# Probabilities times context in three rounded terms, with the sum of exponentials by accumulating transfers

## The chip, the cores and the metric

The kernel runs on one core of one Trainium2 chip. The metric is device time in microseconds; the time before is the median of three runs.

## The reference

Eight batches of 56 tokens with 128 channels attend to 1500 context rows each, with 16 heads of 64, and an expert network follows. All is float32.

```python
x = x + xattn(layernorm(x), ctx, mask, Wq, Wkv, Wout, bout)
#   q = x @ Wq; k, v = split(ctx @ Wkv); 16 heads
#   dots = q k^T * SCALE - (1 - mask[query]) * 1e6
#   out = softmax(dots) v @ Wout + bout
x = x + ffn(layernorm(x), w1, b1, w2, b2)
#   one expert per batch: gelu(x @ w1[e] + b1[e]) @ w2[e] + b2[e]
```

## The kernel before

The weights are folded: the query's and the key's of a head into w_qk, the value's and the output's into w_vo. So attention works on the context itself. A batch has Q = 16 x 56 = 896 query columns `qk`; its 1500 context rows are 12 tiles of 125 (TM, MT).

Scores are made in three rounded terms. A float32 value is cast to float32r (the high part, `ctxt_hi`, `qk_hi`), and the rest is subtracted (`ctxt_lo`, `qk_lo`, on GpSimd). TensorE takes high x high, high x low and low x high, each in two halves c of 448 columns: six matmuls per tile (L398) into one of two PSUM buffers ps_s. Before that, from tile 2 on, ScalarE has written the shift of each query (its maximum and the mask) there (`seed`, L612), so that ScalarE's exponential (L605) gives bounded probabilities `ex`, in a ring of six tiles. For tiles 0 and 1 the shift is a matmul (L412). Probabilities times context (L426, `probs_ctx`) is two float32 matmuls per tile, in the accumulators ps_a. VectorE adds the tiles to `ex_sum` one by one (`add_tile`, L762), and TensorE sums that over partitions with a matrix of ones (L441).

One call of `iteration(b)` on each engine does batch b and in its cracks other work. Step t has three places (t, 0), (t, 1), (t, 2) on TensorE: in the scores of tile t ahead of the third term, behind the scores, and inside the probabilities of tile t-2, which stand last in a step. In the first two steps those are tiles 10 and 11 of the batch before. At the places of MAX_AT stand 21 matmuls (L434) over the next batch's scores, whose maxima VectorE takes (L765). They, the sums, the shift and the expert network are "jobs": each writes one of two PSUM banks ps_x in turn, and waits until the one of two jobs earlier has been read (`job_free`). Every second iteration (a pair of batches done) also has the output projection (L453, at (5, 2)), the norm, and the expert network (L473 at (8, 1), L482 at (11, 2)) of the pair before. Its gelu is exponential, cap, logarithm, exponential and product, on ScalarE in steps 10 and 11 (L655, L661, L663) and on VectorE (L863, at (11, 1)). A loop of three rounds runs iterations 1 to 6 in twos; batch 0 and batch 7 stand outside. Batch 7's second half of a pair follows at the end by itself.

Each engine takes its instructions in the order written. VectorE's per step is `drain((t, 0))`, `between`, the addition of tile t-1, `drain((t, 1))`, `drain((t, 2))`; it also casts the next batch's context (`ctxt_hi_chunk`, L782, in steps 0 and 1) and queries (`qk_hi_part`, L786). In steps 3 and 4 it takes the sums (`drain_sum`, L793) with ScalarE's inverses (L635). GpSimd's only waits are for the high parts. SyncE loads the context twice per batch, as rows (`ctx_sb`, two buffers) and transposed (`ctxt_raw`, one buffer, reloaded when `ctxt_lo` is done).

## Time and profile before

| | us |
|---|---|
| median of three runs | 407.91 (405.58 to 409.17) |
| the profiled execution | 405.75 |
| its span on the core | 403.9 |

The profile is one execution. Its page lists busy time by engine (1), the span in 40 slices with TensorE's granted clock and the transfers (2), the DMA queues (3), the chain of work that ended last, followed back from the last instruction (4), and the costliest groups by line with the wait before them (5). A line number is that of the kernel. PE is TensorE, DVE VectorE, ACT ScalarE, POOL GpSimd, SPq the queue of SyncE. Where several records stand in one row (x6), the duration is that of all of them. A float32 matmul leaves two records, a rounded one leaves one. Matmuls overlap in the records, so the distance from start to start is what one costs.

### The profile page before, as it was taken

To read this page: it belongs to the slowest core of one execution; us is meant where nothing else is said; L and a number is where in the kernel's file an instruction comes from. 1 tells how busy PE (TensorE), PEld (TensorE's weight loads), DVE (VectorE), ACT (ScalarE), POOL (GpSimd) and SP (SyncE) were. 2 spreads that over 40 slices of the span, in tenths; PEclk is the share of its full clock that TensorE was granted. 3 is DMA by queue.
4 is the path that set the end of the run, shared out by engine and by line. 5 is a ranking of instruction groups with operands and counts; after the bars stand their busy time and mean duration, and the time that the engine had idled before them with its cause. 6 is when DMAs were issued, how large, how long until landed. Compare 5 with 4: busy or idle time off the path is not lost.

```text
span 403.9 us, 5555 instructions
## 1 busy us (share of the span) xinstructions
PE 390.0 (97%) x1721; PEld 281.2 (70%) x1721; DVE 302.8 (75%) x490; ACT 206.0 (51%) x274; POOL 57.6 (14%) x47
## 2 busy tenths in 40 slices
PE   7998999999999999999999999999999999999995
PEld 6665666767675877767776877667766777676684
DVE  4889678877887689877887689787887686365443
ACT  3546354565457444665455454565357444746431
POOL 0603400600060000600060001500150000000000
PEclk9999999999999999999999999999999999999999
DMA  7660020040005000042004000160011001100000
GB/s 252 210 199 21 2 76 1 12 142 0 2 4 148 2 2 2 25 155 81 0 18 135 0 0 0 43 193 26 0 35 42 0 0 53 57 2 0 3 2 3
DMA packets 20661, 19.62 MB, mean 49 GB/s; under 512 B 904, under 2 KB 17576, under 8 KB 20648
## 3 DMA queue, kind: packets, MB, share of 16 engines
q1 hardware_dynamic: 20648, 19.45, 15.7%
q8 instruction: 8, 0.13, 0.1%
q14 instruction: 5, 0.04, 0.0%
HBM read 19.21 MB, written 0.23 MB: 48 GB/s over the span
## 4 chain that ended last, share of the span: by engine, by line
PE 90%; DVE 5%; ACT 2%; issue 1%; DMA 1%; SPq 0%; ACTq 0%; DVEq 0%
PE ps_a L426 35%; PE ps_s L398 28%; PE ps_x L434 10%; PE ps_x L453 4%; PE ps_x L441 3%; PE ps_a L373 2%; PE ps_x L473 2%; PE ps_x L482 2%; PE ps_s L412 2%; DMA ex<-in_wk_t 1%; DVE log_sum L793 1%; DVE ctxt_hi L782 1%; ACT inv_sum L635 1%; PE ps_s L528 1%; PE ps_x L412 1%
## 5 line engine op out<-in xcount | busy, mean ns | idle before, releaser
L426 PE MATMUL ps_a<-ex,ctx_sb 125*128 125x448 f32 x384 | 172.1, 541 | 0.0
L605 ACT ACTIVATE ex<-ps_s 125x896 f32<-125x896 f32 x96 | 88.0, 917 | 117.4 <-PE ps_s L398 91.3
L765 DVE TENSOR_REDUCE chunk_max<-ps_x 128x1 f32<-128x500 f32 x168 | 111.3, 674 | 32.6 <-PE ps_x L434 29.5
L434 PE MATMUL ps_x<-ctxt_hi,qk_hi 128*128 128x500 f32 x168 | 88.5, 530 | 6.3 <-DVE log_sum L793 3.6
L426 PEld LDWEIGHTS ps_a<-ex,ctx_sb 125*128 125x128 f32 x384 | 71.4, 189 | 27.5 <-issue 21.6
L762 DVE TENSOR_TENSOR ex_sum<-ex_sum,ex 125x896 f32<-125x896 f32 x80 | 86.6, 1083 | 4.6 <-ACT ex L605 4.6
L398 PE MATMUL ps_s<-qk_hi,ctxt_hi 128*125 128x448 f32 x192 | 87.2, 535 | 0.0
L612 ACT COPY ps_s<-shift_row 125x896 f32<-125x896 f32 x80 | 72.9, 911 | 9.9 <-DVE shift_row L882 7.8
L398 PEld LDWEIGHTS ps_s<-qk_hi,ctxt_hi 128*125 128x125 f32 x192 | 35.8, 187 | 35.5 <-issue 35.1
L398 PE MATMUL ps_s<-qk_hi,ctxt_lo 128*125 128x448 f32 x192 | 57.3, 379 | 0.0
L1008 POOL TENSOR_TENSOR qk_lo<-qk,qk_hi 128x448 fp32r<-128x448 f32 x16 | 23.7, 1483 | 218.9 <-DVE qk_hi L786 218.1
L398 PE MATMUL ps_s<-qk_lo,ctxt_hi 128*125 128x448 f32 x192 | 54.8, 366 | 0.0
L434 PEld LDWEIGHTS ps_x<-ctxt_hi,qk_hi 128*128 128x128 f32 x168 | 31.5, 188 | 26.6 <-issue 9.2
L398 PEld LDWEIGHTS ps_s<-qk_hi,ctxt_lo 128*125 128x125 f32 x192 | 35.6, 186 | 6.9 <-issue 2.6
L398 PEld LDWEIGHTS ps_s<-qk_lo,ctxt_hi 128*125 128x125 f32 x192 | 35.6, 185 | 3.4
L1014 POOL TENSOR_TENSOR ctxt_lo<-ctxt_raw,ctxt_hi 128x500 fp32r<-128x500 f32 x24 | 32.0, 1347 | 11.3 <-DVE ctxt_hi L782 11.3
L782 DVE CAST ctxt_hi<-ctxt_raw 128x500 fp32r<-128x500 f32 x24 | 23.7, 1018 | 0.0
L793 DVE TENSOR_TENSOR log_sum<-ps_x,inv_sum 128x448 f32<-128x448 f32 x16 | 9.3, 619 | 18.6 <-ACT inv_sum L635 18.6
L453 PEld LDWEIGHTS ps_x<-w_vo,att_n 128*128 128x128 f32 (+1 forms) x160 | 18.1, 170 | 1.5 <-issue 1.2
L453 PE MATMUL ps_x<-w_vo,att_n 128*128 128x128 f32 (+1 forms) x160 | 18.6, 275 | 0.0
L629 ACT ACTIVATE log_sum<-ps_x 128x448 f32<-128x448 f32 x16 | 8.7, 542 | 10.7 <-PE ps_x L441 10.6
L648 ACT ACTIVATE logv<-veps 128x1 f32<-128x1 f32 (+2 forms) x7 | 1.4, 204 | 24.7 <-DVE veps L828 22.5
(79 smaller groups left out, 263.3 us busy)
## 6 DMA issues: line engine op xcount, KB each, us to landing
ctxt_raw<-in_ctx_t SPq DMA_DIRECT2D x8, 750.0 KB, 7.4
ctx_sb<-in_ctx SPq DMA_DIRECT2D x8, 750.0 KB
w_sb<-in_w SPq DMA_DIRECT2D x4, 512.0 KB, 3.8
w_sb<-in_w SPq DMA_DIRECT2D x8, 256.0 KB, 4.4
ex<-in_wq_t SPq DMA_DIRECT2D x2, 256.0 KB, 3.9
ex<-in_wk_t SPq DMA_DIRECT2D x2, 256.0 KB, 4.8
att_n<-in_wv_t SPq DMA_DIRECT2D x1, 512.0 KB, 5.9
att_n<-in_w_out SPq DMA_DIRECT2D x1, 512.0 KB, 7.1
```

Source lines behind the costliest of these rows:

```text
L398: mm = nc.tensor.matmul(dst[c], a[:, u, rows], q[:, u, chunks[c]], start=(n == 0 and not seed), stop=(n == 2 and seed), skip_group_check=seed)
L426: mm = nc.tensor.matmul(ps_a[:, c, 0:CH], ctx_sb[0:MT, u, t, :], ex[0:MT, t % RING, c * CH:(c + 1) * CH], start=(t == 0), stop=(t == TM - 1))
L434: nc.tensor.matmul(bank[:, 0:MC], qk_hi[:, u, t * P:(t + 1) * P], ctxt_hi[:, u, k * MC:(k + 1) * MC], start=True, stop=True).then_inc(job_ ...
L453: mm = nc.tensor.matmul(bank[pair.tokens(), 0:D], att_n[:, h, pair.tokens()], w_vo[:, h, :], start=(h == 0), stop=(h == HEADS - 1))
L605: nc.scalar.activation(half(ex[0:MT, slot, :]), src, ACT.Exp, scale=SCALE).then_inc(ex_ready, 1)
L612: nc.scalar.copy(ps_s[0:MT, t % 2, :, 0:CH], half(shift_row[0:MT, :])).then_inc(seeded, 1)
L762: nc.vector.tensor_tensor(dst, left, ex[0:MT, t % RING, :], ALU.add).then_inc(ex_summed, 1)
L765: nc.vector.tensor_reduce(chunk_max[:, k, t:t + 1], filled()[:, 0:MC], AX.X, ALU.max).then_inc(job_free, 1)
L782: nc.vector.tensor_copy(ctxt_hi[:, b.parity, k * MC:(k + 1) * MC], ctxt_raw[:, k * MC:(k + 1) * MC]).then_inc(ctxt_hi_ready, 1)
L793: nc.vector.tensor_tensor(log_sum[:, cols], bank[:, 0:CH], inv_sum[:, cols], ALU.mult).then_inc(job_free, 1)
L1008: nc.gpsimd.tensor_tensor(qk_lo[:, b.parity, cols], b.pick(qk)[:, cols], qk_hi[:, b.parity, cols].bitcast(F32), ALU.subtract).then_inc(qk_ ...
L1014: nc.gpsimd.tensor_tensor(ctxt_lo[:, b.parity, cols], ctxt_raw[:, cols], ctxt_hi[:, b.parity, cols].bitcast(F32), ALU.subtract).then_inc(c ...
```

## The change

For nine of the twelve tiles (SPLIT) probabilities times context is done in rounded terms like the scores. ScalarE takes the exponential of such a tile a second time, into a float32r ring `ex_hi`; VectorE subtracts it from the first (`low_part`, `ex_lo`); GpSimd splits the context rows of these tiles once per batch into `ctx_hi` and `ctx_lo` (`split_ctx`, a copy and a subtraction for four tiles in step 8 of the iteration before, and for five in step 1). TensorE then does six rounded matmuls in place of two float32 ones.

The sum is no longer made by eleven additions. Tiles 0, 1 and 2 are written into `ex_first` (two copies, by parity), which are three accumulators. GpSimd issues a transfer for each of the tiles 3 to 10 (in the last batch 3 to 8) that adds the tile to the accumulator t % 3 (`add_by_dma`), after the transfer before it on that accumulator has landed. VectorE adds tile 11 and the other two accumulators to the third, at (0, 1), (1, 0) and (1, 2) of the next iteration. Tiles 3 to 11 go through a ring of four, and an exponential waits for the transfer that reads its slot. The full 128 partitions are transferred, so both are cleared at the start.

The query cast moves from VectorE to ScalarE, behind the exponential of tile 0. The context casts stand all in step 0. `shifts` is one place earlier. In MAX_AT the place (3, 2) is no longer used, and the tables of GpSimd's work (CTXT_LO_AT, QK_LO_AT) are changed: its queue now waits for the exponentials of each step. `hid` and its two companions lie in `w_qk`'s memory.

```diff
-    RING = 6
-    assert D == P and MT * TM == M and QT * P == Q and MC * KM == M and E == B and TM % RING == 0
-    CTXT_LO_AT, QK_LO_AT = [2, 6, 7], [2, 3]
+    RING, ACCS, LAST_DMA = 4, 3, 10
+    assert D == P and MT * TM == M and QT * P == Q and MC * KM == M and E == B and ACCS < RING < LAST_DMA < TM
+    SPLIT = [1, 2, 4, 5, 6, 7, 8, 9, 10]
+    PARTS = 3
+    assert len(SPLIT) % PARTS == 0 and 0 not in SPLIT and TM - 1 not in SPLIT
+    CTXT_LO_AT, QK_LO_AT = [5, 6, 7], [2, 9]
+    CTX_SPLIT_AT = [8, 1]
     REFINE_AT, ATT_N_AT, Z_AT = (3, 3), (4, 3), (6, 2)
-    QK_HI_AT = (0, 0)
-    CTXT_HI_AT = [(0, 1), (0, 2), (1, 0)]
+    CTXT_HI_AT = [(0, 0), (0, 1), (0, 2)]
+    SUM_PARTS_AT = [(0, 1), (1, 0), (1, 2)]
+    LAST_SUM_PARTS_AT = [(9, 2), (10, 0), (10, 2), (11, 0)]
     MAX_AT = [
-        [(1, 1), (1, 2), (2, 0), (2, 1), (2, 2), (3, 2), (4, 0), (4, 2), (5, 0), (5, 2), (6, 0),
-         (6, 1), (6, 2), (7, 0), (8, 0), (8, 2), (9, 0), (9, 1), (9, 2), (10, 1), (10, 2)],
-        [(1, 1), (1, 2), (2, 0), (2, 1), (2, 2), (3, 2), (4, 0), (4, 2), (5, 0), (5, 2), (6, 0),
-         (6, 2), (7, 0), (7, 1), (8, 0), (8, 1), (8, 2), (9, 1), (9, 2), (10, 1), (10, 2)],
+        [(1, 1), (1, 2), (2, 0), (2, 1), (2, 2), (4, 0), (4, 1), (4, 2), (5, 0), (5, 1), (6, 0),
+         (6, 2), (7, 0), (7, 1), (8, 0), (8, 2), (9, 0), (9, 2), (10, 0), (10, 1), (10, 2)],
+        [(1, 1), (1, 2), (2, 0), (2, 1), (2, 2), (4, 0), (4, 1), (4, 2), (5, 0), (5, 2), (6, 0),
+         (6, 2), (7, 0), (7, 2), (8, 0), (8, 2), (9, 0), (9, 2), (10, 0), (10, 1), (10, 2)],
     ]
...
-        ex = sb("ex", [P, RING, Q])
-        ex_sum = sb("ex_sum", [P, 2, Q])
+        ex_first = sb("ex_first", [P, 2, ACCS, Q])
+        ex_ring = sb("ex_ring", [P, RING, Q])
+        ex_hi = sb("ex_hi", [P, PARTS, Q], F32R)
+        ex_lo = sb("ex_lo", [P, PARTS, Q], F32R)
+        ctx_hi = sb("ctx_hi", [P, len(SPLIT), D], F32R)
+        ctx_lo = sb("ctx_lo", [P, len(SPLIT), D], F32R)
...
+        ADDS = [sum(t % ACCS == j for t in range(ACCS, LAST_DMA + 1)) for j in range(ACCS)]
+        DVE_SUMS = TM - 1 - LAST_DMA + ACCS - 1
+        LAST_BATCH_DMA = 8
...
+        def last_dma(b):
+            return LAST_BATCH_DMA if b.off == B - 1 else LAST_DMA
+        def sums_of(b):
+            return TM - 1 - last_dma(b) + ACCS - 1
+        def ex(b, t):
+            return ex_first[:, b.parity, t, :] if t < ACCS else ex_ring[:, (t - ACCS) % RING, :]
+        def parts_free(eng, b, t):
+            n = SPLIT.index(t)
+            if n >= PARTS:
+                eng.wait_ge(pv_done, b.at(TM, SPLIT[n - PARTS] + 1))
+            elif b.i is not None or b.off > 0:
+                eng.wait_ge(pv_done, b.later(-1).at(TM, SPLIT[n - PARTS] + 1))
+        def dma_added(eng, b, t):
+            eng.wait_ge(ex_added[t % ACCS], b.at(16 * ADDS[t % ACCS], 16 * (t // ACCS)))
...
-                for c in range(2):
-                    if c == 1 and between is not None:
-                        between()
-                    mm = nc.tensor.matmul(ps_a[:, c, 0:CH], ctx_sb[0:MT, u, t, :], ex[0:MT, t % RING, c * CH:(c + 1) * CH],
-                                          start=(t == 0), stop=(t == TM - 1))
+                if t in SPLIT:
+                    n = SPLIT.index(t)
+                    pe.wait_ge(ex_hi_ready, b.at(len(SPLIT), n + 1))
+                    if t in (SPLIT[0], SPLIT[4]):
+                        pe.wait_ge(ctx_lo_ready, b.at(2, 1 if t == SPLIT[0] else 2))
+                    for k, (w, e) in enumerate([(ctx_hi, ex_hi), (ctx_lo, ex_hi), (ctx_hi, ex_lo)]):
+                        if k == 1 and between is not None:
+                            between()
+                        if k == 2:
+                            pe.wait_ge(ex_lo_ready, b.at(len(SPLIT), n + 1))
+                        for c in range(2):
+                            mm = nc.tensor.matmul(ps_a[:, c, 0:CH], w[0:MT, n, :], e[0:MT, n % PARTS, c * CH:(c + 1) * CH],
+                                                  start=False, stop=False)
+                else:
+                    for c in range(2):
+                        if c == 1 and between is not None:
+                            between()
+                        mm = nc.tensor.matmul(ps_a[:, c, 0:CH], ctx_sb[0:MT, u, t, :], ex(b, t)[0:MT, c * CH:(c + 1) * CH],
+                                              start=(t == 0), stop=(t == TM - 1))
...
-                wait(act, pv_done, b.at(TM, t - RING + 1))
-                wait(act, ex_summed, b.at(TM - 1, max(t - RING, 1)) if t >= RING else b.at(TM - 1, t - RING + 1))
-                nc.scalar.activation(half(ex[0:MT, slot, :]), src, ACT.Exp, scale=SCALE).then_inc(ex_ready, 1)
+                if t >= ACCS + RING:
+                    act.wait_ge(pv_done, b.at(TM, t - RING + 1))
+                    dma_added(act, b, t - RING)
+                elif t >= ACCS and (b.i is not None or b.off > 0):
+                    act.wait_ge(pv_done, b.at(TM, 0))
+                    before = b.later(-1)
+                    last = max(s for s in range(ACCS, TM) if (s - t) % RING == 0)
+                    if last <= LAST_DMA:
+                        dma_added(act, before, last)
+                    else:
+                        act.wait_ge(ex_summed, before.at(DVE_SUMS, last - LAST_DMA))
+                nc.scalar.activation(half(ex(b, t)[0:MT, :]), src, ACT.Exp, scale=SCALE).then_inc(ex_ready, 1)
+            def high_part(b, t):
+                parts_free(act, b, t)
+                nc.scalar.activation(half(ex_hi[0:MT, SPLIT.index(t) % PARTS, :]), ps_s[0:MT, t % 2, :, 0:CH], ACT.Exp,
+                                     scale=SCALE).then_inc(ex_hi_ready, 1)
+            def qk_hi_part(b):
+                wait(act, scores_ready, b.at(TM, -TM))
+                nc.scalar.copy(qk_hi[:, b.parity, :], b.pick(qk)).then_inc(qk_hi_ready, 1)
...
+                if t - 2 in SPLIT:
+                    act.wait_ge(ex_hi_ready, b.at(len(SPLIT), SPLIT.index(t - 2) + 1))
...
+                    if t in SPLIT:
+                        high_part(b, t)
                     if t == 1 and b.off > 0:
                         att_out(b.later(-1))
+                    if t == 0 and prepare:
+                        qk_hi_part(b.later(1))
...
+            def sum_parts(b):
+                end = last_dma(b)
+                tiles = [(t, max(s for s in range(end + 1) if s % ACCS == ACCS - 1)) for t in range(end + 1, TM)]
+                chains = [(j, max(s for s in range(end + 1) if s % ACCS == j)) for j in range(ACCS - 1)]
+                return chains + tiles if b.off == B - 1 else tiles + chains
+            def add_to_sum(b, n):
+                dst = ex_first[0:MT, b.parity, ACCS - 1, :]
+                t, dma = sum_parts(b)[n]
+                if n == 0:
+                    dma_added(dve, b, max(s for s in range(last_dma(b) + 1) if s % ACCS == ACCS - 1))
+                if t > last_dma(b):
+                    dve.wait_ge(ex_ready, b.at(TM, t + 1))
+                else:
+                    dma_added(dve, b, dma)
+                wait(dve, ex_summed, b.at(DVE_SUMS, n))
+                nc.vector.tensor_tensor(dst, dst, ex(b, t)[0:MT, :], ALU.add).then_inc(ex_summed, 1)
+            def low_part(b, t):
+                n = SPLIT.index(t)
+                parts_free(dve, b, t)
                 dve.wait_ge(ex_ready, b.at(TM, t + 1))
-                dst = ex_sum[0:MT, b.parity, :]
-                left = ex[0:MT, 0, :] if t == 1 else dst
-                if t > 1:
-                    dve.wait_ge(ex_summed, b.at(TM - 1, t - 1))
-                nc.vector.tensor_tensor(dst, left, ex[0:MT, t % RING, :], ALU.add).then_inc(ex_summed, 1)
+                dve.wait_ge(ex_hi_ready, b.at(len(SPLIT), n + 1))
+                nc.vector.tensor_tensor(ex_lo[0:MT, n % PARTS, :], ex(b, t)[0:MT, :], ex_hi[0:MT, n % PARTS, :].bitcast(F32),
+                                        ALU.subtract).then_inc(ex_lo_ready, 1)
...
-                    if prepare and at == QK_HI_AT:
-                        qk_hi_part(b.later(1))
                     if prepare and at in CTXT_HI_AT:
                         ctxt_hi_chunk(b.later(1), CTXT_HI_AT.index(at))
+                    if b.off > 0 and at in SUM_PARTS_AT:
+                        add_to_sum(b.later(-1), SUM_PARTS_AT.index(at))
+                    if at[0] - 1 in SPLIT and at[1] == 1:
+                        low_part(b, at[0] - 1)
+                    if not prepare and at in LAST_SUM_PARTS_AT:
+                        add_to_sum(b, LAST_SUM_PARTS_AT.index(at))
                     if b.off > 0 and at == REFINE_AT:
                         refine_inverse()
                     if b.off > 0 and at == ATT_N_AT:
...
                         gelu_cap(pair)
                     if pair is not None and at == (HID_AT[0] + 3, 1):
                         gelu(pair)
-                    if prepare and at == (TM - 1, 1):
+                    if prepare and at == (TM - 1, 0):
...
+            def add_by_dma(b, t):
+                pool.wait_ge(ex_ready, b.at(TM, t + 1))
+                if t < 2 * ACCS:
+                    pool.wait_ge(pv_done, b.at(TM, t % ACCS + 1))
+                else:
+                    dma_added(pool, b, t - ACCS)
+                pool.sem_inc(add_may_go, 1)
+                pool.dma_start(ex_first[:, b.parity, t % ACCS, :], ex(b, t), accum_op=ALU.add).then_inc(ex_added[t % ACCS], 16)
+            def split_ctx(b, g):
+                if g == 0:
+                    pool.wait_ge(ctx_in[b.parity], b.at_every_other(16, 16))
+                    parts = lambda w: w[0:MT, 0:4, :].rearrange("p (i j) d -> p i j d", j=2)
+                    raw = ctx_sb[0:MT, b.parity, 1:7, :].rearrange("p (i j) d -> p i j d", j=3)[:, :, 0:2, :]
+                else:
+                    parts = lambda w: w[0:MT, 4:9, :]
+                    raw = ctx_sb[0:MT, b.parity, 6:11, :]
+                if b.i is not None or b.off > 0:
+                    pool.wait_ge(pv_done, b.later(-1).at(TM, SPLIT[3 if g == 0 else 8] + 1))
+                pool.sem_inc(ctx_may_split, 1)
+                nc.gpsimd.tensor_copy(parts(ctx_hi), raw).then_inc(ctx_hi_ready, 1)
+                pool.wait_ge(ctx_hi_ready, b.at(2, g + 1))
+                nc.gpsimd.tensor_tensor(parts(ctx_lo), raw, parts(ctx_hi).bitcast(F32), ALU.subtract).then_inc(ctx_lo_ready, 1)
             def iteration(b, prepare=True):
                 for t in range(TM):
+                    if ACCS < t <= last_dma(b) + 1:
+                        add_by_dma(b, t - 1)
+                    if t == CTX_SPLIT_AT[1]:
+                        split_ctx(b, 1)
+                    if prepare and t == CTX_SPLIT_AT[0]:
+                        split_ctx(b.later(1), 0)
...
+            nc.gpsimd.memset(ex_first[:, :, :, :].rearrange("p u r q -> p (u r q)")[:, 2 * HP * P:], 0.0).then_inc(ex_cleared, 1)
+            nc.gpsimd.memset(ex_ring[:, :, :], 0.0).then_inc(ex_cleared, 1)
+            split_ctx(Batch(None, 0), 0)
```

## Rows read from the trace of the kernel before

**Rows 1.** The page, parts 1 and 2: busy us (share) xinstructions; granted TensorE clock by slice.
```profile
PE 390.0 (97%) x1721; PEld 281.2 (70%) x1721; DVE 302.8 (75%) x490; ACT 206.0 (51%) x274; POOL 57.6 (14%) x47
...
PEclk9999999999999999999999999999999999999999
```

**Rows 2.** The page, part 4: shares of the chain that ended last, by line.
```profile
PE ps_a L426 35%; PE ps_s L398 28%; PE ps_x L434 10%; PE ps_x L453 4%; PE ps_x L441 3%; PE ps_a L373 2%; PE ps_x L473 2%; PE ps_x L482 2%; PE ps_s L412 2%; DMA ex<-in_wk_t 1%; DVE log_sum L793 1%; DVE ctxt_hi L782 1%; ACT inv_sum L635 1%; PE ps_s L528 1%; PE ps_x L412 1%
```

**Rows 3.** DMA view: packets, MB, share of 16 engines; issues, KB each, us to landing.
```profile
q1 hardware_dynamic: 20648, 19.45, 15.7%
...
x_tok<-in_x SPq DMA_DIRECT2D x1, 256.0 KB, 2.7
```

**Rows 4.** Groups of instructions by line: busy us, mean ns, then idle before.
```profile
L765 DVE TENSOR_REDUCE chunk_max<-ps_x 128x1 f32<-128x500 f32 x168 | 111.3, 674 | 32.6 <-PE ps_x L434 29.5
```

**Rows 5.** The chain inside one pair iteration: start us, us, what, records.
```profile
207.64 0.23 PE ps_x L434
...
212.84 1.52 PE ps_x L441 x4
...
216.10 0.50 PE ps_x L434
216.60 0.76 PE ps_a L426 x2
...
245.35 1.22 PE ps_s L398 x6
...
247.32 1.51 PE ps_x L482 x16
```

**Rows 6.** Two whole iterations: us, busy PE, PEld, DVE, ACT, POOL; clock, DMA. Second: pair.
```profile
160.10:201.40 41.30, 40.71 (x153) 28.31 (x152) 33.70 (x47) 22.76 (x27) 6.96 (x5) 1.00 0.19 64
201.40:249.50 48.10, 47.50 (x218) 34.76 (x216) 38.99 (x64) 24.87 (x32) 6.96 (x5) 1.00 0.11 32
```

**Rows 7.** Waits of the whole span: us in total, times, longest.
```profile
ACT ex L605 <- PE ps_s L398: 91.3, 65, 3.6
...
PE ps_x L434 <- DVE log_sum L793: 3.6, 6, 0.6
```

**Rows 8.** Timeline of VectorE, then of GpSimd: start us, us, instruction.
```profile
201.38 0.62 DVE L786 CAST qk_hi<-qk 128x896 fp32r x1
201.92 1.08 DVE L762 TENSOR_TENSOR ex_sum<-ex_sum,ex 125x896 f32<-125x896 f32 x1
202.92 1.36 DVE L782 CAST ctxt_hi<-ctxt_raw 128x500 fp32r<-128x500 f32 x1
...
215.42 1.16 DVE L793 TENSOR_TENSOR log_sum<-ps_x,inv_sum 128x448 f32<-128x448 f32 x2 [1.88 <-ACT inv_sum L635]
...
246.22 0.69 DVE L863 TENSOR_TENSOR hid<-hid,hid_u 128x512 f32<-128x512 f32 x1
...
202.19 1.82 POOL L1008 TENSOR_TENSOR qk_lo<-qk,qk_hi 128x448 fp32r<-128x448 f32 x1 [33.92 <-DVE qk_hi L786]
204.36 1.26 POOL L1014 TENSOR_TENSOR ctxt_lo<-ctxt_raw,ctxt_hi 128x500 fp32r<-128x500 f32 x1 [0.36 <-DVE ctxt_hi L782]
```

**Rows 9.** Timeline of ScalarE around gelu in a pair iteration.
```profile
240.30 0.92 ACT L605 ACTIVATE ex<-ps_s 125x896 f32<-125x896 f32 x1 [3.01 <-PE ps_s L398]
241.25 0.91 ACT L612 COPY ps_s<-shift_row 125x896 f32<-125x896 f32 x1
242.09 0.63 ACT L655 ACTIVATE hid_e<-hid_u 128x512 f32<-128x512 f32 x1
...
244.97 0.63 ACT L663 ACTIVATE hid_u<-hid_e 128x512 f32<-128x512 f32 x1
```

**Rows 10.** The tile ctxt_raw: ns min/median/max; us from issue to landing.
```profile
L782 DVE CAST ctxt_hi<-ctxt_raw x24: 411/1358/1372, 10.1 to 295.2; 128x500 fp32r<-128x500 f32 x24
...
DMA to landing us min/median/max: 4.1/7.4/11.4
```

**Rows 11.** The line of the memset on GpSimd: ns min/median/max.
```profile
L1022 POOL MEMSET att_n<- x1: 1808/1808/1808, 45.7 to 45.7; 128x2048 f32 x1
```

29 lines of the change are left out of this document (13 added, 16 removed).

## The prediction

> **What bounds the kernel now.** I read the page from the top. The busy line [rows 1] has TensorE at 390.0 of 403.9 us, VectorE at 75%, ScalarE at 51%, GpSimd at 14%; the granted clock is 9 tenths or more in all 40 slices, the higher of the two levels (2.4 GHz), so nothing of what follows comes from the clock. Busy time alone proves little for matmuls, so the chain that ended last comes next [rows 2]: its TensorE items add up to some 90%, and the largest, 35%, is L426, probabilities times context. Transfers use a sixth of the sixteen engines' time [rows 3]. The chain followed inside one pair iteration [rows 5] gives the price of each piece and shows how densely they follow each other. The reader should take three prices from it. Six rounded matmuls of 448 columns (the scores of a tile) take 1.22 us, 0.203 each. One float32 matmul of 448 columns, which the trace keeps as two records, takes 0.75 to 0.76, so a tile's two take 1.51. A matmul for a maximum takes 0.23. The windows of whole iterations [rows 6] say the same: TensorE has 40.7 busy in 41.3 us, and 47.5 in 48.1 with a pair. VectorE has 33.7 of the 41.3, ScalarE 22.8: room on both, but on VectorE not much.
>
> **What TensorE saves.** In a split tile, two float32 matmuls (1.51) give way to six rounded ones (6 x 0.203 = 1.22): 0.29 less. There are 9 split tiles in each of 8 batches: 72 x 0.29 = 20.9 us, all of it on the chain. This is the surest term, since the six scores matmuls have the same 448 columns, a weight load each, and the same packing as the new ones. Tiles 0, 3 and 11 keep 1.51.
>
> **A hole that closes.** The max at (3, 2) stands behind the two sum matmuls and needs banks that VectorE frees after ScalarE's logarithms and exponentials. In [rows 5] the sum matmuls end at 214.36; 0.41 of scores and 0.75 of L426 later the max could have started and ended at 215.75, yet the chain leaves it at 216.60: 0.85 us, in each of six iterations (the waits list has L434 behind log_sum six times [rows 7]). The new MAX_AT has no job at (3, 2); the next is at (4, 0), 0.41 + 1.22 + 0.81 = 2.44 after the sums, while the second drain ended 2.2 after them (215.42 + 1.16 [rows 8]). The margin is 0.2, so I book most of it: -4 (bounds 0 and -5.1).
>
> **ScalarE.** Added: a second exponential per split tile, 9 x 0.95 (start to start in [rows 9], 240.30 to 241.25), and the query cast, one 896-wide instruction; no row has it, it lies between nothing and another 0.95, and by its width I take 0.95. Together 9.5 us on top of 22.8: 32.3 in about 38.5. What it delays must be asked place by place. The usual tile: scores(t+2) needs seed(t+2), which now stands behind the exponential and the high part: 3 x 0.95 and 0.3 of latency, 3.15 after the end of scores(t). TensorE has probabilities 1.22, scores 1.22, probabilities 1.22 and four max jobs (0.9) between: 4.6. Hidden, with 1.4 to spare. In the last batch there are no maxima: TensorE needs 2.44 per tile and ScalarE 2.85; over tiles 5 to 10 it falls 2.5 behind and has 1.2 to 1.5 of slack: +1 (bounds 0 and +2.5).
> The place where it isn't hidden is gelu. Count in [rows 9] from the start of exp 9 (240.30): seed from 0.95, the gelu exponential until 2.4, exp 10, logarithm and exponential until 5.3, VectorE's product (L863 [rows 8]) until 6.6, the output matmul from 7.0 [rows 5]. Afterwards: exp, high part, seed until 2.8, gelu exponential 3.4, exp 10 and its high part 5.3, logarithm and exponential 6.6, product 7.3. TensorE comes there sooner. From the end of scores(9), 0.3 before exp 9: max 0.23, probabilities 1.22, scores 1.22, three max 0.69, probabilities 1.22, scores 1.22, a third of probabilities 0.41: 6.2, so 5.9 on this count. A new wait of 1.4 to 1.5, in three pair iterations and in the last one (half the width): 4 x 1.5 = +6 (bounds 0, if the order of work leaves slack that I don't see, and +8). Behind the waiting output job are the rest of probabilities(9) and the next iteration's scores.
>
> **VectorE.** Removed: 11 additions per batch (L762, 1.00 from start to start [rows 8]) and the query cast (0.62). Added: 9 low parts of the same form and width, and 3 additions. 33.7 + 1.0 - 0.6 = 34.1 before contention, in 38.5 us: 88% where it had 82%. The context casts of step 0 came 1.36 long where the shortest took 0.41 [rows 10]; GpSimd's L1008 was at work then [rows 8]. Now GpSimd is paced by its new waits and has nothing to do in step 0, and up to 1.9 us of that comes back. Against it, GpSimd's reads now fall among low parts and adds. What a meeting costs stands in [rows 8]: L1008, 448 columns, took 1.82 when it started under L762, and by L1014's 1.26 for 500 columns it should take 1.13: 0.7. GpSimd gains two copies and two subtractions per batch (512 and 640 columns); the subtractions take 2.9 by L1014; the copies lie between the memset's 0.9 ns a column [rows 11] and the subtraction's 2.5, so 1.0 to 2.9. That makes nine GpSimd instructions of 0.5 to 1.6 us per iteration; if half of them meet a two-input instruction of VectorE and cost it 0.7, that is 3 us, and VectorE ends at 32 to 37 of 38.5. It doesn't set the time on average, but there are only two banks, and single max jobs will come late. I book 0.4 per iteration: +3 (bounds 0 and +10).
> By the Trainium skill (SBUF — State Buffer, Who interferes with whom) the port pair that VectorE and GpSimd share is an exclusive lock, which a VectorE instruction with two SBUF inputs also takes against a GpSimd instruction that reads. The rows above agree in both directions. By it all of the low parts can be blocked, which is the first rival's case.
>
> **Transfers.** Eight of them per batch (tiles 3 to 10; six in the last), 128 x 3584 bytes = 0.459 MB, each read, added to its target in SBUF and written. The trace has none. 19.45 MB took 15.7% of the engines' span [rows 3], 63.4 us of all sixteen: 307 GB/s. One pass is 1.5 us, two (the target is read as well) 3.0, three 4.5; I take 3.0. The fixed part: x_tok's 0.26 MB landed after 2.7 us [rows 3], 1.85 above its 0.85. Their deadline: tile 3's exponential ends some 15 us into an iteration, and VectorE wants tile 10's chain at (1, 2) of the next, about 46 in. 31 us, less 2 of latency and 2.4 for the context load in that stretch, is 3.3 per transfer. Exp(t) waits for the transfer of t-4, four tiles or 11 us before it, and the three chains leave 8.6 us for each. Cost 0, hidden behind TensorE's tiles. GpSimd must also issue them; even at 1 us each it stays under 60% busy.
> ctxt_raw is reloaded only after the last low chunk, now in step 7, where GpSimd was done with it in the first steps. The load is wanted four and a half steps, 12.6 us, later, and landed in 4.1 to 11.4 [rows 10], the long ones together with the ctx_sb load, from which it is now apart. Hidden; else VectorE's step 0 is late. The two clearing memsets (6912 columns, 6.1 us at 1.81 for 2048 [rows 11]) run beside the first batch's maxima. Hidden.
>
> **Sum.** Own time of the profiled execution: 405.75. -20.9 - 4 + 1 + 6 + 3 = -14.9, to 390.9. The median of the runs shown is 2 above that execution, so I say 391.
>
> **Rivals.**
> VectorE and GpSimd block each other until VectorE sets the pace. For: 88% before any contention, and nine low parts with a deadline. Against: the maxima (L765) read PSUM and kept a mean of 0.67 [rows 4]. With 1 to 1.5 lost per iteration instead of 0.4: 396 to 400.
> The transfers come late (the slower side). Place: VectorE's add at (1, 2), behind it every max of the iteration, and TensorE for its banks. It decides from 3.3 us per transfer. At 4.0, 0.7 x 8 = 5.6 per iteration, seven times: 39 us, 430; at three passes 458. For: nothing in the trace gives the rate of an adding transfer. Against: the middle bound fits.
> The Trainium skill (DMA: Bandwidth & Descriptors, Anatomy of one DMA) has 2.0 us plus bytes over 436 GB/s for a transfer issued by GpSimd; an estimate from it is 3.05 for 0.459 MB with the latency in it, with which the sum would stand as it is. No run here shows it yet.
> ScalarE paces the split tiles in the other batches too (2.85 against 2.44 plus maxima, 2.9 to 3.1): 0.2 a tile, six tiles, eight batches, 10 us: 400. Against: it waits 91 us for scores [rows 7].
> Nothing gained, the six matmuls costing what the two did (0.25 each): 412. Against: the scores row.
> All covers hold, no gelu wait and no contention: 381.
>
> **Numbers.** Forecast (386 to 395) 0.45; better, 381 to 386, 0.13; VectorE paced 0.15 and ScalarE paced 0.10 (both 396 to 403 for the most part); transfers late 0.14; nothing gained 0.03. Range 381 to 408. A measurement of this kernel can tell about 1% from no change: faster (under 403.8) 0.72, within 0.10, slower 0.18.
>
> **What would show it.** L426's rounded group at 0.2 us per matmul on the chain, 1.22 per split tile; no wait of L434 for log_sum; the output matmul (L482) waiting 1.5 for L863's product, four times; VectorE 85 to 95% busy in an iteration and ScalarE near 83%; transfers landing within 5 us, with no wait of VectorE for them; iterations of 38 to 39 us, 46.5 with a pair. I am wrong if a transfer takes over 7 us, if GpSimd's instructions stretch to 2 us throughout, or if scores wait for seeds.

## The result and the profile after

The changed kernel takes 423.9 us (median of four runs, 422.5 to 426.8) where the kernel before takes 407.8 on the same chip (405.6 to 409.2). The ratio is 1.043, 95% interval 1.039 to 1.048: 16 to 18 us slower. The prediction was 391. The ratios below leave out one slow execution, of e10.

The first look is the page of the changed kernel: busy time of each engine, the granted clock of TensorE by slice, the queue of the adding transfers, and the chain by engine.

```profile
PE 383.6 (90%) x1865; PEld 313.5 (74%) x1865; DVE 329.4 (78%) x493; ACT 269.0 (63%) x353; POOL 155.8 (37%) x143
...
PEclk9999999999999998999999999999999998999699
...
q0 software_dynamic: 8928, 28.45, 36.2%
...
PE 57%; DVE 23%; issue 13%; ACT 3%; DMA 3%; DVEq 1%; SPq 0%; ACTq 0%; POOLq 0%
```

Against [rows 1] TensorE is 6 us less busy in a span 21 us longer, and VectorE has 27 us more busy time for three instructions more. The chain, some nine tenths TensorE before [rows 2], now runs over VectorE for 23%. Next comes the list of waits of the changed kernel (engine, tile and line, releaser: us in total, times, longest).

```profile
PEld ps_x L490 <- DVE chunk_max L867: 24.6, 28, 2.3
...
PE ps_x L538 <- DVE w_qk L962: 17.3, 5, 6.2
PE ps_x L490 <- DVE chunk_max L867: 16.1, 20, 1.9
```

These are two places. L490 is the matmul for a maximum; it waits for the bank that VectorE's reduction (L867) frees. L538 is the expert network's output matmul for a pair of batches; it waits for the product that ends gelu (L962). The wait of the maximum for log_sum in [rows 7] is gone. Two whole iterations of the changed kernel, the second with a pair (us, then busy PE, PEld, DVE, ACT, POOL; clock, DMA share, GB/s), stand against [rows 6]:

```profile
161.00:206.00 45.00, 42.62 (x191) 35.07 (x192) 36.70 (x49) 30.74 (x37) 19.79 (x17) 0.96 0.60 134
206.00:255.50 49.50, 43.62 (x214) 35.36 (x212) 42.82 (x63) 32.88 (x42) 18.17 (x17) 1.00 0.53 110
```

I cut the span at the first and the last start of the instruction that begins the shifts (776 before, 878 after). Up to the first there are 29.9 us before and 33.0 after; the seven iterations between take 307.1 and 314.6; what follows takes 67.0 and 77.3. The first of the three differences isn't the change: it moves between 29.7 and 33.5 from run to run, and the kernel before with nothing but another list of maxima (e4, below) has 32.9 there. So the loss is in the seven iterations, which should have become some 18 us shorter and became 7.6 longer, and in the last batch, 10.4 longer.

**VectorE beside GpSimd.** This is the changed kernel's timeline (start us, us, instruction), first VectorE, then GpSimd, then TensorE:

```profile
236.03 0.15 DVE L916 TENSOR_SCALAR corr<-rstd 128x1 f32<-128x1 f32 x1
236.22 1.99 DVE L917 TENSOR_TENSOR rstd<-corr,rstd 128x1 f32<-128x1 f32 x1
238.24 0.35 DVE L932 TENSOR_SCALAR z<-x,meanvar,rstd 128x128 f32<-128x128 f32 x1
238.50 0.67 DVE L867 TENSOR_REDUCE chunk_max<-ps_x 128x1 f32<-128x500 f32 x1
...
236.02 0.88 POOL L1124 DMA_DIRECT2D ex_first<-ex_ring  x1 [5.34 <-ACT ex_ring L669]
236.63 1.54 POOL L1113 TENSOR_TENSOR ctxt_lo<-ctxt_raw,ctxt_hi 128x500 fp32r<-128x500 f32 x1
...
239.23 0.49 PE L490 MATMUL ps_x<-ctxt_hi,qk_hi 128*128 128x500 f32 x1 [1.91 <-DVE chunk_max L867]
```

L917 multiplies one column. Its shortest form takes 0.15 us, its median 0.16; here it takes 1.99 and ends at 238.21, where GpSimd's subtraction ends (236.63 + 1.54 = 238.17). The reduction behind it keeps its 0.67, only starts late, and TensorE stands still for 1.91. L917's record starts 0.42 us before that of the subtraction, beside a transfer's issue (L1124). The issue isn't what holds it: in e3 and e10 below L917 stands beside the same issue and takes 0.16.

I counted over the whole trace the VectorE instructions that are more than 0.15 us above the shortest of their line, tiles and form: 40 (39 of them stand alone in the timeline), together 32.7 us too long, and every one of them lies beside a GpSimd copy or subtraction. None lies beside a transfer's issue (0.88 us each) alone. The kernel before has 20 such, 14.6 us, all of them context casts (L782) that took up to 1.37 where the shortest took 0.41 [rows 10]. So the two engines met before the change as well, some 2 us in each iteration, but at casts, and VectorE had only 5% of the chain. After it the casts are short again, and what is held up is additions, low parts and the normalisation (L906: 2.54 us in the median, 1.09 without a meeting).

**Gelu.** The changed kernel's timeline at the end of a pair iteration, ScalarE, VectorE, TensorE:

```profile
253.26 0.63 ACT L740 ACTIVATE w_qk<-w_qk 128x512 f32<-128x512 f32 x1
...
254.44 1.09 DVE L878 TENSOR_TENSOR shift_diag<-ident,row_max 128x896 fp32r<-128x896 f32 x1
255.44 1.09 DVE L863 TENSOR_TENSOR ex_lo<-ex_ring,ex_hi 125x896 fp32r<-125x896 f32 x1
256.45 0.69 DVE L962 TENSOR_TENSOR w_qk<-w_qk 128x512 f32<-128x512 f32 x1
...
257.28 1.55 PE L538 MATMUL ps_x<-w_sb,w_qk 128*64 128x128 f32 x16 [3.08 <-DVE w_qk L962]
```

ScalarE's last exponential ends at 253.9. The product L962 needs nothing else, but starts at 256.45: ahead of it in VectorE's queue stand the shifts (from 253.7) and the low part of tile 10. All three pairs inside show 3.08 or 3.09.

**The last batch.** The same two timelines of the changed kernel, VectorE's and TensorE's, and behind them its windows (columns as above):

```profile
391.06 2.29 DVE L855 TENSOR_TENSOR ex_first<-ex_first 125x896 f32<-125x896 f32 x2 [4.46 <-DMA ex_first<-ex_ring]
393.26 1.09 DVE L863 TENSOR_TENSOR ex_lo<-ex_ring,ex_hi 125x896 fp32r<-125x896 f32 x1
394.26 0.29 DVE L956 TENSOR_SCALAR w_qk<-w_qk 128x256 f32<-128x256 f32 x1
394.46 2.28 DVE L855 TENSOR_TENSOR ex_first<-ex_first,ex_ring 125x896 f32<-125x896 f32 x2
...
397.67 0.42 DVE L962 TENSOR_TENSOR w_qk<-w_qk 128x256 f32<-128x256 f32 x1
...
398.23 1.94 PE L538 MATMUL ps_x<-w_sb,w_qk 128*64 128x128 f32 x8 [6.24 <-DVE w_qk L962]
```

```profile
394.00:398.00 4.00, 0.00 (x0) 0.00 (x0) 3.90 (x6) 1.64 (x3) 0.00 (x0) 0.75 0.00 0
398.00:400.00 2.00, 1.77 (x8) 1.57 (x8) 0.09 (x1) 0.00 (x0) 0.00 (x0) 0.50 0.00 0
400.00:402.00 2.00, 2.00 (x6) 1.73 (x6) 1.28 (x2) 0.00 (x0) 0.00 (x0) 0.50 0.05 14
402.00:404.00 2.00, 2.00 (x8) 1.67 (x8) 0.00 (x0) 0.00 (x0) 0.00 (x0) 0.80 0.00 0
```

VectorE's first addition at (9, 2) waits 4.46 us for the last adding transfer; the low part, gelu's cap and its product are queued behind that and behind two double additions. TensorE waits 6.24. During this wait its granted clock falls to 0.50, the lower level (1.2 GHz), and it stays there until 402.8, for 4.6 us of work: L538's eight matmuls take 1.94, against 1.06 in e2 below.

### The profile page after: what moved, and what is told of

It is laid out like the page before. It is cut to its first block, busy times and chain, and to the rows that moved or that the text cites. A ratio compares the mean times of both kernels' runs of the same rounds, so it can differ in the third digit from the quotient of the medians.

```text
span 425.0 us, 6363 instructions
## 1 busy us (share of the span) xinstructions
PE 383.6 (90%) x1865; PEld 313.5 (74%) x1865; DVE 329.4 (78%) x493; ACT 269.0 (63%) x353; POOL 155.8 (37%) x143
## 4 chain that ended last, share of the span: by engine, by line
PE 57%; DVE 23%; issue 13%; ACT 3%; DMA 3%; DVEq 1%; SPq 0%; ACTq 0%; POOLq 0%
PE ps_s L440 15%; PE ps_a L476 11%; PE ps_x L490 7%; PE ps_a L482 7%; DVE chunk_max L867 5%; PE ps_x L509 4%; DVE ex_lo L863 4%; PE ps_x L497 3%; DVE ex_first L855 2%; PE ps_x L538 2%; PE ps_a L413 2%; DVE inv_sum L899 2%; PE ps_x L529 1%; DVE rstd L917 1%; DMA ex_first<-ex_ring 1%
## 5 line engine op out<-in xcount | busy, mean ns | idle before, releaser
L867 DVE TENSOR_REDUCE chunk_max<-ps_x 128x1 f32<-128x500 f32 x168 | 109.1, 671 | 16.7 <-PE ps_x L490 14.4
L1124 POOL DMA_DIRECT2D ex_first<-ex_ring x62 | 54.2, 874 | 150.8 <-ACT ex_ring L669 142.6
L669 ACT ACTIVATE ex_ring<-ps_s 125x896 f32<-125x896 f32 x72 | 66.1, 917 | 41.2 <-PE ps_s L440 35.8
L490 PE MATMUL ps_x<-ctxt_hi,qk_hi 128*128 128x500 f32 x168 | 76.7, 459 | 16.4 <-DVE chunk_max L867 16.1
L863 DVE TENSOR_TENSOR ex_lo<-ex_ring,ex_hi 125x896 fp32r<-125x896 f32 x56 | 69.6, 1243 | 2.5 <-ACT ex_hi L674 2.5
L674 ACT ACTIVATE ex_hi<-ps_s 125x896 fp32r<-125x896 f32 x72 | 65.8, 913 | 0.0
L440 PE MATMUL ps_s<-qk_hi,ctxt_hi 128*125 128x448 f32 x192 | 63.6, 413 | 0.1
L490 PEld LDWEIGHTS ps_x<-ctxt_hi,qk_hi 128*128 128x128 f32 x168 | 31.4, 188 | 33.8 <-DVE chunk_max L867 24.6
L669 ACT ACTIVATE ex_first<-ps_s 125x896 f32<-125x896 f32 x24 | 22.1, 921 | 34.2 <-PE ps_s L454 34.0
L476 PE MATMUL ps_a<-ex_hi,ctx_lo 125*128 125x448 f32 x144 | 43.4, 384 | 0.0
L476 PE MATMUL ps_a<-ex_lo,ctx_hi 125*128 125x448 f32 x144 | 42.1, 375 | 0.0
L476 PE MATMUL ps_a<-ex_hi,ctx_hi 125*128 125x448 f32 x144 | 41.8, 372 | 0.0
L476 PEld LDWEIGHTS ps_a<-ex_hi,ctx_lo 125*128 125x128 f32 x144 | 27.5, 197 | 3.9 <-issue 1.2
L476 PEld LDWEIGHTS ps_a<-ex_lo,ctx_hi 125*128 125x128 f32 x144 | 27.9, 194 | 2.4
```

The source lines that it names most:

```text
L440: mm = nc.tensor.matmul(dst[c], a[:, u, rows], q[:, u, chunks[c]], start=(n == 0 and not seed), stop=(n == 2 and seed), skip_group_check=seed)
L476: mm = nc.tensor.matmul(ps_a[:, c, 0:CH], w[0:MT, n, :], e[0:MT, n % PARTS, c * CH:(c + 1) * CH], start=False, stop=False)
L490: nc.tensor.matmul(bank[:, 0:MC], qk_hi[:, u, t * P:(t + 1) * P], ctxt_hi[:, u, k * MC:(k + 1) * MC], start=True, stop=True).then_inc(job_ ...
L669: nc.scalar.activation(half(ex(b, t)[0:MT, :]), src, ACT.Exp, scale=SCALE).then_inc(ex_ready, 1)
L674: nc.scalar.activation(half(ex_hi[0:MT, SPLIT.index(t) % PARTS, :]), ps_s[0:MT, t % 2, :, 0:CH], ACT.Exp, scale=SCALE).then_inc(ex_hi_read ...
L863: nc.vector.tensor_tensor(ex_lo[0:MT, n % PARTS, :], ex(b, t)[0:MT, :], ex_hi[0:MT, n % PARTS, :].bitcast(F32), ALU.subtract).then_inc(ex_ ...
```

## The experiments

Three causes stand to be told apart, called A, B and C from here on: the loss comes from VectorE instructions that GpSimd's reads hold up (A), from VectorE's queue order ahead of gelu's product and in the last batch (B), and from the clock, which follows on long waits (C). The rivals to A and B were that ScalarE or the transfers cost the time. Each kernel is compared with the kernel before on the same chip. "Ratio" is to that; a difference of two ratios times 406 gives us. The ratio isn't the quotient of the two medians, and such a difference is uncertain by 2 to 3 us, from the intervals.

**e1: the product ahead of the shifts.** One place changed in VectorE's program.

```diff
-                    if pair is not None and at == (HID_AT[0] + 3, 1):
+                    if pair is not None and at == (HID_AT[0] + 3, 0):
                         gelu(pair)
```

> The changed kernel with gelu's product (L962) taken by VectorE at (11, 0), ahead of the shifts and of the last low part. Theory O (the order in VectorE's queue makes the output matmul wait): the wait of 3.08 us in each of three pair iterations falls by the two instructions groups ahead of it (0.7 and 1.1 for the shifts, 1.0 for the low part), 2.6 each, and the long wait of 6.24 in the last batch by 1.0 or 2: 9 us less, about 415. Rival S (ScalarE's second exponentials make the logarithm and exponential of gelu late, as the prediction had it): VectorE would then stand waiting for them, and the gain is under 3 us.

Measured: 417.04, ratio 1.022 (1.016 to 1.027), 8.8 us below the changed kernel (6.9 by the medians). L538's waits fall from 17.3 us to 8.3, the three inner ones from 3.08 to 0.58; a pair iteration and a plain one together take 92.2 where they took 94.7 and 93.1. The waits of L490 stay (16.0). So gelu's wait was VectorE's queue: with ScalarE's work untouched, four fifths of the inner waits go.

**e2: the last batch.** One adding transfer less, the additions later and in another order.

```diff
-    LAST_SUM_PARTS_AT = [(9, 2), (10, 0), (10, 2), (11, 0)]
+    LAST_SUM_PARTS_AT = [(9, 2), (10, 2), (10, 3), (11, 1), (11, 2)]
-        LAST_BATCH_DMA = 8
+        LAST_BATCH_DMA = 7
-                return chains + tiles if b.off == B - 1 else tiles + chains
+                return tiles[:1] + chains + tiles[1:] if b.off == B - 1 else tiles + chains
```

> The changed kernel with one transfer less in the last batch (tiles 3 to 7) and VectorE's adds of it spread over (9, 2), (10, 2), (10, 3), (11, 1), (11, 2). Theory L: in the last batch VectorE stands 4.46 us at the add for tile 8's transfer, the output matmul behind it 6.24, and TensorE's clock falls to the lower level for about 6 us after it. Without that wait 4 to 5 us of the stand and 2.3 of the slow clock go: 6 to 7 less, about 417.5. Rival: the stand is filled by another wait of the same chain (ScalarE's exponentials): 2 us or less.

Measured: 422.86, ratio 1.041 (1.035 to 1.048): about 1 us, no difference that can be told; 6 to 7 was expected, and the rival's 2 or less fits the number but not the reason. In the profile the last wait did shrink from 6.24 to 2.83 us, L538's eight matmuls take 1.06, and what follows the last shifts is 3.9 us shorter (73.4 against 77.3). The seven iterations before it are 2.7 us longer (317.4 against 314.6); e2's windows (columns as above) and its first output matmul show where.

```profile
158.00:161.00 3.00, 0.00 (x0) 0.00 (x0) 2.87 (x4) 0.54 (x1) 0.00 (x0) 0.86 0.72 134
161.00:163.00 2.00, 1.92 (x13) 1.95 (x14) 0.00 (x0) 0.00 (x0) 0.00 (x0) 0.50 0.00 0
163.00:168.00 5.00, 5.00 (x19) 4.24 (x17) 2.04 (x4) 0.00 (x0) 0.00 (x0) 0.60 0.00 0
```

```profile
161.08 2.85 PE L538 MATMUL ps_x<-w_sb,w_qk 128*64 128x128 f32 x16 [3.08 <-DVE w_qk L962]
```

In this 3.08 us wait the clock fell before L538 and stayed low until 167.0: L538 takes 2.85 us, 1.70 at this place in the changed kernel, where the clock fell only at 163.9, and 1.55 at the full clock. In all TensorE works 16.1 us at the lower level in e2 and 11.4 in the changed kernel; at half the clock that is 2.4 us more. A wait of this length is followed by the lower level in some places and not in others: nothing fell behind the one that ends at 257.28. Only with the inner waits gone as well (e6) does this edit show what it is worth.

**e3: GpSimd made silent.** The low parts of query and context and the context split are cut to four columns from batch 2 on; the waits, their order and the transfers stay.

```diff
-                cols = slice(c * CH, (c + 1) * CH)
+                cols = slice(c * CH, (c + 1) * CH if b.i is None and b.off < 2 else c * CH + 4)
...
-                cols = slice(k * MC, (k + 1) * MC)
+                cols = slice(k * MC, (k + 1) * MC if b.i is None and b.off < 2 else k * MC + 4)
...
+                if b.i is not None or b.off > 1:
+                    parts = lambda w: w[0:MT, 4 * g, 0:4]
+                    raw = ctx_sb[0:MT, b.parity, 1 + 5 * g, 0:4]
```

> The changed kernel with GpSimd's subtractions and copies cut to 4 columns each from batch 2 on (the low parts of context, transposed context and queries of later batches are left out); its transfers and its waits stay. Theory P (an instruction of GpSimd that reads holds up any two-input instruction of VectorE that meets it): the 39 lengthened instructions and their 32 us vanish, TensorE's waits for maxima (17.8) with them and the restarts after them: 15 to 20 us less, 404 to 409. Rival V (VectorE has too much work by count, twelve wide instructions against eleven and the casts): the lengthened ones cost little, and it is 5 us or less.

Measured: 408.5, ratio 1.005 (1.002 to 1.009), 15.4 us below the changed kernel. VectorE is busy 298.1 us instead of 329.4, with the same instructions; four are lengthened (2.3 us), in the first batches, where GpSimd's work is whole, instead of 40 (32.7). The waits of e3:

```profile
PE ps_x L538 <- DVE w_qk L962: 16.9, 5, 5.8
...
PE ps_x L490 <- DVE chunk_max L867: 3.7, 7, 0.7
```

L490's waits fall from 16.1 to 3.7 and L538's stay: A and B are two separate causes. These 12.4 us are most of the 15.4; 1.7 more are waits of L509 for maxima, which are gone too. The 62 adding transfers run as before in e3, so they are not what holds VectorE.

**e4: the kernel before with the new list of maxima.** Before's MAX_AT in both forms is replaced by the changed kernel's (no job at (3, 2)).

```diff
-        [(1, 1), (1, 2), (2, 0), (2, 1), (2, 2), (3, 2), (4, 0), (4, 2), (5, 0), (5, 2), (6, 0),
+        [(1, 1), (1, 2), (2, 0), (2, 1), (2, 2), (4, 0), (4, 1), (4, 2), (5, 0), (5, 1), (6, 0),
...
```

> The kernel before, with the changed kernel's table MAX_AT, which has no job at (3, 2), and nothing else of the change. Theory H (the hole of 0.85 us behind the sums closes): 6 x 0.7 to 0.85, 4 to 5 us less than before, about 403.5. Rival: the work that fills the hole is missing elsewhere, or other jobs come to stand behind it: within 1 us of before.

Measured: 405.77, ratio 0.995 (0.993 to 0.998), 1.9 us (0.9 by the medians), where 4 to 5 was expected. The wait for log_sum is gone from the list, as the prediction had it, but the hole was worth less than its 0.85 us in each iteration: pair iterations stay at 47.2 us and a new wait of the output matmul appears in them. e4's timeline of TensorE:

```profile
159.62 1.55 PE L482 MATMUL ps_x<-w_sb,hid 128*64 128x128 f32 x16 [0.63 <-DVE hid L863]
```

The chain of gelu through ScalarE and VectorE is as long as before; TensorE only comes to it earlier.

**e6: e1 and e2 together.** The two edits above, and nothing else.

> The changed kernel with gelu's product at (11, 0) and one transfer less in the last batch; all is computed. The gain of the product alone was 6.9, of the last batch alone 1 (4 us in its own stretch, part of it lost elsewhere to a fall of TensorE's clock behind the gelu waits). With those waits at 0.6 the clock should not fall, and 10 us go: 414. If the last batch's gain is a matter of chance, 417.

Measured: 410.14, ratio 1.009 (1.006 to 1.013), 13.8 us below the changed kernel; L538 waits 4.4 us in all, L490 15.9 as ever. From e1 to e6 e2's edit is worth 5.0 us, where alone it showed 0.9; the intervals alone couldn't tell these two apart, but in the profiles what follows the last shifts goes from 71.0 to 65.0. The kernel is faster than the 414 expected. That the clock would not fall, though, was wrong: it fell three times, each time behind a wait of 1.91 us of a maximum (L490), the one that the held-up L917 makes. e6's TensorE and its windows (columns as above):

```profile
141.34 0.49 PE L490 MATMUL ps_x<-ctxt_hi,qk_hi 128*128 128x500 f32 x1 [1.91 <-DVE chunk_max L867]
```

```profile
142.70:146.10 3.40, 3.40 (x12) 2.96 (x10) 1.65 (x5) 0.00 (x0) 1.87 (x2) 0.50 0.99 249
```

So A too is paid a second time through the clock.

**e5: e1, e2 and e3 together.** It leaves out what e3 leaves out.

> Three edits together: gelu's product at (11, 0), one transfer less in the last batch, and GpSimd's reading instructions cut to 4 columns from batch 2 on (the low parts of later batches are left out). If order, last batch and held-up VectorE are what the change lost, the gains add: 423.9 - 15 (as measured alone) - 7 - 3 = 399 or less, below the kernel before (406.6), and an iteration without a pair takes 38.5, with one 43 or less, which is what the prediction had for the saving of 0.29 us per split tile. If the rounded matmuls themselves bring less than 0.29 per tile, it stays at 403 or more.

Measured: 390.7, ratio 0.964 (0.959 to 0.969). This is the time the prediction had, and it is reached with both causes taken away. That the two numbers meet is chance: the predicted 391 holds 6 us for gelu, where e5 still waits 3.3 inside (L538), 3 for VectorE, whose meetings are gone here, and -4 for a hole that gave 2 (e4). Without a pair an iteration takes 39.7 and with one 45.7, where 38.5 and 43 were expected of this run. e5's page, then its windows (columns as above), then its chain (start us, us, what, records):

```profile
PE 372.1 (96%) x1865; PEld 308.6 (80%) x1865; DVE 298.6 (77%) x494; ACT 268.4 (69%) x353; POOL 102.5 (26%) x142
...
PEclk9999999999999999999999999999999999999999
```

```profile
151.20:190.90 39.70, 39.20 (x184) 32.53 (x182) 32.42 (x47) 30.12 (x37) 10.29 (x17) 1.00 0.65 148
190.90:236.60 45.70, 44.31 (x225) 37.12 (x224) 37.12 (x63) 33.33 (x43) 10.72 (x17) 1.00 0.59 123
```

```profile
155.33 1.22 PE ps_a L476 x6
156.55 1.23 PE ps_s L440 x6
...
162.79 0.75 PE ps_a L482 x2
```

The six rounded matmuls of a tile's probabilities (L476) take 1.22, the two float32 ones of an unsplit tile 0.75 each: the saving of 0.29 per tile is there. ScalarE is busy 30.1 of 39.7 us and doesn't hold the others up. From e3 to e5 the same two edits bring 16.7 us, where on top of the changed kernel they bring 13.8. L538's waits are 11.8 of the 16.7; e3 still has a mean clock of 0.973 where e5 has 0.997 (middle of each one's runs). In e3's profile TensorE works 13.6 us at the lower level, in and behind three of the waits of L538, and in e5's none before its last matmul: at half the clock that is 6.8 us, which covers the 5 that are left of the 16.7. So these are put down to C; no run changes the clock alone.

**e7 and e8: two remedies for A that leave nothing out.** Both stand on e6. e7 cuts each reading instruction of GpSimd in pieces (four for a low part, one context tile each for the split); e8 leaves them whole and moves them to the first steps of an iteration.

```diff
 e7, for query and context low parts alike:
-                cols = slice(k * MC, (k + 1) * MC)
-                nc.gpsimd.tensor_tensor(ctxt_lo[...], ...).then_inc(ctxt_lo_ready, 1)
+                w = MC // 4
+                for m in range(4):
+                    cols = slice(k * MC + m * w, k * MC + (m + 1) * w)
+                    ins = nc.gpsimd.tensor_tensor(ctxt_lo[...], ...)
+                ins.then_inc(ctxt_lo_ready, 1)
 e8:
-    CTXT_LO_AT, QK_LO_AT = [5, 6, 7], [2, 9]
+    CTXT_LO_AT, QK_LO_AT = [0, 1, 2], [0, 1]
```

> The same as the kernel with both order edits, and each of GpSimd's subtractions and copies cut into pieces: 112 and 125 columns in place of 448 and 500, one tile of 128 columns at a time for the context. The work is the same. Theory P: a two-input instruction of VectorE waits for the end of the GpSimd instruction that it meets, so pieces of 0.3 us hold it up for 0.3 at most in place of 1.8; of the 32 us of lengthening some 20 go, and TensorE's waits for maxima halve: 6 to 8 less than without the pieces. Rival: the two engines alternate, so that VectorE meets a piece again and again, or the pieces cost GpSimd more than they free: no gain or slower.

> The same as the kernel with both order edits, and GpSimd's low parts of transposed context and queries in steps 0 to 2 (as they ran before the change) in place of steps 2 and 5 to 9. Theory: before the change the same instructions cost nothing, since they ran beside VectorE's casts and copies; there they would hold up fewer low parts, 3 to 6 less. Rival: steps 0 to 3 already hold five adds, low parts and normalisations with two inputs and the context split of step 1, so it only moves: within 2 us, or slower.

Measured: e7 396.18, ratio 0.974 (0.971 to 0.977); e8 395.25, ratio 0.974 (0.970 to 0.979). Each brings some 14 us on e6, and each is faster than the kernel before. That is twice what was expected of e7 (6 to 8) and more than twice of e8 (3 to 6): the sizes were missed, the direction wasn't. In e7 31 VectorE instructions are lengthened, 13.3 us in all, and L490 waits 10.0 us. In e8 there are 30, 22.5 us, but they fall on low parts and additions that have time in the first steps, and L490 waits 6.5. In neither does the clock fall before the last matmul, so part of the 14 is C. What a meeting costs thus hangs on two things, how long GpSimd's instruction is and what is queued behind the VectorE instruction that it holds.

**e10 and e11: each remedy on the changed kernel alone,** without e1 and e2.

> The changed kernel with nothing but GpSimd's low parts of transposed context and queries put back into steps 0 to 2, two lists of numbers. Theory P: the place of these five instructions was the largest single loss, 15 us on top of the order edits; alone it brings 12 to 15: 409 to 412. Rival: its gain needs the order edits (the 3 us stands behind gelu absorb it): under 8.

> The changed kernel with nothing but GpSimd's reading instructions in pieces. Theory P: 14 us on top of the order edits, so about 10 to 14 alone: 410 to 414, with lengthened VectorE instructions falling from 32 us to 15. Rival: under 8.

Measured: e10 410.22, ratio 1.010 (1.008 to 1.012); e11 411.14, ratio 1.017 (1.011 to 1.023; one of its four runs took 416.0, and by the medians it is 1.013). So two lists of numbers (e10) give back 13.5 us of the change, and the pieces 10.6. L538 keeps its 17 us in both. The eight combinations as ratios:

| GpSimd's reads | as changed | with e1 and e2 |
|---|---|---|
| as changed | 1.043 | 1.009 |
| cut to four columns | 1.005 (e3) | 0.964 (e5) |
| early | 1.010 (e10) | 0.974 (e8) |
| in pieces | 1.017 (e11) | 0.974 (e7) |

Down each column A is worth 11 to 18 us, across each row B (with C) 14 to 18. They add up, nearly.

**e9: early and in quarters.** e7 and e8 together.

> Both order edits, the low parts of GpSimd in steps 0 to 2, and all of GpSimd's reading instructions in pieces of 112 to 128 columns. Alone on the order edits, the pieces brought 14 us and the early place 15; the floor with GpSimd's reads gone is 390.7. Theory P: both act on the same 32 us of lengthening, so together they come near the floor: 391 to 394. Rival: in steps 0 to 3 pieces and two-input instructions alternate and delay the low parts of queries and context: no better than either alone, 395 to 396.

Measured: 394.71, ratio 0.974 (0.971 to 0.976), no better than either, as the rival had it. The lengthening is down to 5.2 us and L490's wait to 3.8, but GpSimd itself is held up. e9's timelines of GpSimd, ScalarE and TensorE:

```profile
198.67 2.60 POOL L1109 TENSOR_TENSOR qk_lo<-qk,qk_hi 128x112 fp32r<-128x112 f32 x4 [4.95 <-ACT qk_hi L680]
...
88.40 2.65 POOL L1130 DMA_DIRECT2D ex_first<-ex_ring  x3
...
96.71 0.92 ACT L669 ACTIVATE ex_ring<-ps_s 125x896 f32<-125x896 f32 x1 [4.04 <-DMA ex_first<-ex_ring]
...
99.43 0.67 PE L440 MATMUL ps_s<-qk_hi,ctxt_hi 128*125 128x448 f32 x2 [2.21 <-ACT ps_s L689]
```

Four quarters of 112 columns take 2.6 us, where 448 columns in one take 1.14 at the shortest in the changed kernel and 1.46 in the median. So GpSimd comes late to its adding transfers, and issues three in a row from 88.4. The exponential that needs a slot of the ring waits 4.04 us for one of them, and the scores behind it wait 2.21 for their seed. There are three such waits of scores in e9, 3.9 us in all, at 99, 186 and 272, and none in e8 and e12. Of the rivals of the prediction, the late transfers are thus the one that the remedy brings in.

**e12: early and in halves.** e8, with the low parts in two pieces each and the context split tile by tile.

```diff
-                cols = slice(k * MC, (k + 1) * MC)
+                w = MC // 2
+                for m in range(2):
+                    cols = slice(k * MC + m * w, k * MC + (m + 1) * w)
```

> As the kernel with order edits, early place and pieces, but the low parts of queries and transposed context in two pieces each (224 and 250 columns, 0.6 us) in place of four; the context split stays one tile at a time. If only the length of the piece that VectorE meets counts, it stands between the early kernel (395.3) and the one in four pieces, 393 to 395; if the split of the context in step 1 was what mattered, it equals the four pieces.

Measured: 390.15 (389.65 to 390.34), ratio 0.961 (0.960 to 0.963), 15.7 us faster than the kernel before with all of the work in it. Neither expectation gave this: 393 to 395, or the 394.7 of the quarters. That it is as fast as e5, which leaves work out, nobody had foreseen. e12's page:

```profile
PE 372.8 (96%) x1865; PEld 308.2 (79%) x1865; DVE 304.3 (78%) x494; ACT 268.3 (69%) x353; POOL 199.3 (51%) x294
...
PEclk9999999999999999999999999999999999999999
```

GpSimd is busier than with whole instructions (199 us against the changed kernel's 156 and e8's 166) and less busy than with quarters (221 to 226 in e7, e9 and e11); VectorE is 25 us less busy than in the changed kernel. 20 lengthened instructions, 7.7 us; L490 waits 4.6, L538 5.0. The three parts of its span are 30.1, 293.3 and 65.0; before they were 29.9, 307.1 and 67.0. The transfers come in time again: where e9 issues three in a row from 88.4, e12 issues two from 85.5; its exponentials wait 0.8 us for transfers in all, e9's 9.6, and its scores never wait for a seed. e9's 3.9 us of such waits are more than the 2.6 between the two profiled executions, and most of the 4.6 between the medians.

## Why the prediction was wrong, point by point

**The saving on TensorE: right.** 0.203 per rounded matmul was read off the scores and holds for the new ones (1.22 for six). 72 x 0.29 = 20.9 us less on TensorE is there in every kernel that has the change; in the changed one waits and the lower clock cover it, in e5 and e12 it comes out, less what gelu takes. In e5 the seven iterations are 15.3 us shorter than before, of 18.3 that 63 tiles make.

**VectorE and GpSimd, booked at +3: the step that failed most.** The prediction saw the block in [rows 8] and counted half of nine GpSimd instructions in an iteration, at 0.7 us each: 3 us of lengthening. That was low, but not by much. In the six whole iterations inside, 5 to 7 VectorE instructions are lengthened, by 4.1 to 5.5 us, 5.0 on average (in the whole span 32.7 / 40 = 0.82 each, up to 1.83). The step that failed is the next one, from these 3 us to the time: "it doesn't set the time on average", 0.4 per iteration, +10 at most. Taking the reads away gives 15.4 us (e3), 18.4 on top of e6; e3's 15.4, spread over seven iterations, are 2.2 each. So the lengthening was short by a factor of 1.7, and the share of it that reaches TensorE by more than three.

Two things made this share large. The 0.7 was read off GpSimd's own instruction, under a wide addition of VectorE; narrow instructions of VectorE with two SBUF inputs are held as well (L917, one column, three times). L906 and L917, of the normalisation and the norm, are held by 1.44 and 1.83, and the maxima stand right behind them. And the time was judged by an average, a share of 88%, where the two banks of L490 look at the single delay.

By the Trainium skill (SBUF — State Buffer, Who interferes with whom) a VectorE instruction with two SBUF inputs takes an exclusive lock against GpSimd's; the runs agree, since all 40 lie beside a GpSimd instruction that reads and in the changed kernel transfers' issues alone hold up none. Not all of the 40 have two inputs: four are casts, as all 20 were before.

The rival that VectorE and GpSimd block each other was the right one as to mechanism, but its 396 to 400 was priced at 1 to 1.5 per iteration. The argument against it, that the maxima read PSUM and keep their mean of 0.67, was true ([rows 4]: 0.674, now 0.671) and of no use: a reduction that keeps its length is late all the same when what stands before it is long. And the prediction called GpSimd's new pace a gain, since it has nothing to do in step 0. The casts did come back to 0.41, but they had cost nothing: in steps 5 to 9 GpSimd's reads lie where maxima are due. Moving them into steps 0 to 2 is worth 13.5 us (e10).

**Gelu, booked at +6: the right place, the wrong queue.** It counted ScalarE's queue and came to 1.4 to 1.5 per pair. ScalarE is done at 253.9, and VectorE's product starts at 256.45, for the `shifts` moved one place up now stand ahead of it, and so does the low part of tile 10. Both moves were in the diff. Three waits of 3.08 and one of 6.24 are 15.5 us, and e1 and e2 together give back 13.8 (e6); the last wait adds the additions and their wait for a transfer, of which the prediction had nothing. With the product ahead of the shifts 0.58 is left in three of four (e1). The fifth wait of L538, 1.82 at the very end, was there before.

**The clock: missed.** "Nothing of what follows comes from the clock" was true of the profile before [rows 1], with TensorE never idle for long. (Of the kernel before's 19 runs beside e1 to e4, those with a mean clock of 0.998 or more took 405.3 to 406.6, and those with 0.993 to 0.996 took 407.6 to 408.7.) The change brought waits of 1.9 to 6.2 us, and in or behind some of them the granted clock fell to 0.50. In the changed kernel there are three such places before the last matmul, and these are its windows there (columns as above):

```profile
163.90:167.30 3.40, 3.40 (x11) 2.76 (x10) 2.04 (x4) 0.00 (x0) 0.00 (x0) 0.50 0.00 0
351.60:355.00 3.40, 3.40 (x11) 2.77 (x10) 1.37 (x2) 0.00 (x0) 0.00 (x0) 0.50 0.06 17
396.00:402.80 6.80, 4.57 (x15) 4.01 (x16) 3.37 (x5) 0.26 (x1) 0.00 (x0) 0.50 0.02 4
```

TensorE works 11.4 us in them at half the clock, which costs an estimated 5.7 us: C is as large as the whole gelu term of the prediction. e6 has three places of 3.4 us behind waits of 1.91, and e3 and e2 have 13.6 and 16.1 us of such work. e5, e7, e8, e9 and e12, where no wait on L490 is over 1.4 us and none on L538 over 0.9 but for the 1.82 at the very end, have no slice below 9.

**The hole, booked at -4: too much.** The wait is gone (right), but e4 has 1.9 us for it, 3.0 at the end of its interval. In pair iterations gelu's chain took it back, which the prediction, with the gelu count on its own page, could have put together.

**ScalarE: right.** The query cast takes 0.93 (0.95 booked). In the changed kernel ScalarE still waits 35.8 us for scores at L669, where it waited 91.3 [rows 7], so it doesn't pace the split tiles; that rival falls. Nor did scores wait for seeds.

**The transfers: right but for one.** The tile view of the issue line in the changed kernel:

```profile
L1124 POOL DMA_DIRECT2D ex_first<-ex_ring x62: 853/877/1010, 45.3 to 385.0; - x62
...
DMA to landing us min/median/max: 4.2/4.9/8.7
```

4.9 us from issue to landing was estimated at 4.85. All sixteen engines together gave 0.362 x 425 / 62 = 2.5 us to each (booked 3.0), below the 3.3 at which they would have been late, so the rival on the slower side falls too, though its sign came true by other means. An estimate from the Trainium skill (DMA: Bandwidth & Descriptors, Anatomy of one DMA) was 3.05; the trace has 4.9, and it decides. The miss is the last batch, where the addition at (9, 2) came 4.46 us before the last transfer had landed: the cover was worked out for batches with a successor only. ctxt_raw's reload landed in 4.9 to 7.6 and held VectorE up nowhere; the casts of step 0 are back at 0.41 (median; 1.36 in [rows 10]), as said. The two memsets took 2.87 + 3.08 = 5.95 (booked 6.1), ended at 26.7, and were hidden.

**What stays open.** In e5 and e12 some 2 us of the predicted 20.9 and of the hole are not accounted for by waits that I can name. Why the lower clock follows on one wait of 1.91 or 3.08 us and not on the next was not tested.

## What to carry to other kernels

Before GpSimd gets elementwise work beside a busy VectorE, list every VectorE instruction with two SBUF inputs, narrow ones too, and every float32 cast out of SBUF that can run at the same time; each may be held until the GpSimd instruction ends, so keep these short and put them where what is queued behind VectorE isn't due. When an operation is moved up in a queue, ask of each waiting consumer in that queue what now stands ahead of it. Price a contention by the delay of the next deadline, not by the engine's busy share, and remember that a wait of 2 to 3 us can be paid a second time through TensorE's clock.

## What the runs showed of the hardware

- A VectorE tensor_tensor on a single column took 1.99 us instead of 0.16, and ended within 0.04 us of the GpSimd subtraction of 500 columns beside it.
- A cast of 500 columns on VectorE took 1.36 instead of 0.41 beside GpSimd's subtractions, 14.6 us over the kernel before, and cost it no time that shows.
- The block goes both ways: GpSimd's subtraction of 500 columns took 1.24 at its shortest and 1.71 at its longest in the changed kernel, and a context split in 72 single tiles plus low parts in halves keeps GpSimd busy 199 us (e12) where the whole ones at the same places take 166 (e8).
- TensorE's granted clock fell to 0.50 in a wait of 6.24 us, in one of 3.08 (e2) and behind ones of 1.91 (e6), and was still 1.00 after another of 3.08.
- An adding SBUF-to-SBUF transfer of 448 KB took 0.88 us to issue on GpSimd, 4.9 us to land, and in the changed kernel slowed no VectorE instruction. In e7 and e11 L917 takes 0.38 instead of 0.16 three times beside such an issue, with a piece of GpSimd's subtraction starting as it ends.
- Six rounded matmuls of 448 columns in place of two float32 ones save 0.29 us of 1.51, at the price of one more exponential (0.91), one subtraction on VectorE (1.08) and a split context.
